# Q and K of a head pair in two row tiles from split operands, in a transformer block whose VectorE, ScalarE and TensorE orders are written by hand

## What is computed

```python
x = x + 0.5 * ffn(layernorm(x), w_gate, w_up, w_down)          # 128 -> 352 -> 128, silu(gate) * up
x = x + attn(layernorm(x), w_q, w_k, w_v, w_proj, b_proj, ln_gamma, ln_beta)
x = x + 0.5 * ffn(layernorm(x), w_gate, w_up, w_down)

# attn(x): 16 heads of 64
q, k, v = (split_heads(x @ w) for w in (w_q, w_k, w_v))
attn = softmax(einsum('bnqd,bnkd->bnqk', q, k) * 64 ** -0.5)
o = einsum('bnqk,bnkd->bnqd', attn, v)
y = o @ w_proj + b_proj + x;  y = layernorm(y, eps=1e-6) * ln_gamma + ln_beta
```

## Time and profile before

| | |
|---|---|
| Three runs | 2266.74, 2265.52, 2261.74 us, median 2265.52 |
| Profiled execution, its own time | 2263.16 us |
| Its span | 2261.4 us, 38387 instructions |
| TensorE matmul busy | 2142.7 us (95%) |
| VectorE, GpSimd, ScalarE busy | 1605.5, 1407.7, 1151.4 us (71%, 62%, 51%) |
| Mean granted TensorE clock | 0.978 |
| Costliest on TensorE | PV 552.3 us, Q and K 267.1 us, V 137.5 us, projection 126.7 us, row sums 68.2 us |

### The profile page before, as it was taken

The page is one execution under the profiler, slowest core; times in us unless marked ns, Lnnn a source line. Parts: engine busy times, 40 slices in busy tenths (PEclk is TensorE's granted clock), DMA queues, the critical chain, the costliest instruction groups (busy, mean ns, idle before and its releaser), DMA issues.

```text
span 2261.4 us, 38387 instructions
## 1 busy us (share of the span) xinstructions
PE 2142.7 (95%) x14537; PEld 1094.4 (48%) x14537; DVE 1605.5 (71%) x2609; ACT 1151.4 (51%) x1749; POOL 1407.7 (62%) x1289
## 2 busy tenths in 40 slices
PE   3899999999999999999999999999999999999974
PEld 2344444545445454545545454554544545454432
DVE  5565767767687786868777686877778687776634
ACT  2455554645555454555545455455555545454532
POOL 3365666757576675757756576675757667665642
PEclk8799999999999999999999999999999999999986
DMA  1000000000000000000000000000000000000000
GB/s 60 1 7 2 6 2 2 12 2 7 7 7 7 2 11 2 7 7 7 7 2 11 2 7 7 2 12 2 10 3 6 7 2 12 2 2 7 2 7 10
DMA packets 167493, 15.83 MB, mean 7 GB/s; under 512 B 148304, under 2 KB 166928, under 8 KB 167312
## 3 DMA queue, kind: packets, MB, share of 16 engines
q1 hardware_dynamic: 167312, 13.39, 5.1%
HBM read 7.03 MB, written 4.19 MB: 5 GB/s over the span
## 4 chain that ended last, share of the span: by engine, by line
PE 85%; DVE 6%; SPq 2%; issue 2%; POOL 2%; DMA 1%; ACT 1%; POOLq 0%; DVEq 0%
PE pS L934 23%; PE pO L961 20%; PE pM L918 9%; PE pX L946 5%; PE pM L1077 5%; PE pX L985 5%; PE pM L973 3%; PE LpF L333 2%; PE FpF L333 2%; SPq L568 2%; PE FpF L296 2%; PE LpF L296 2%; PE LpF L309 2%; PE FpF L309 2%; PE LpF L324 1%
## 5 line engine op out<-in xcount | busy, mean ns | idle before, releaser
L676 POOL TENSOR_TENSOR ES<-ES,E 128x512 f32<-128x512 f32 x512 | 654.9, 1300 | 217.1 <-ACT E L747 209.9
L747 ACT ACTIVATE E<-pS 128x1024 f32<-128x1024 f32 x512 | 523.2, 1022 | 459.9 <-PE pS L934 421.3
L799 DVE TENSOR_REDUCE nmax<-pX 128x2 fp32r<-128x1024 f32 x512 | 622.0, 1215 | 113.4 <-PE pX L946 98.4
L961 PE MATMUL pO<-E,VA 128*64 128x512 f32 x2048 | 552.3, 618 | 0.0
L670 POOL TENSOR_TENSOR ES<-E 128x512 f32<-128x512 f32 x256 | 321.9, 1279 | 247.5 <-ACT E L747 247.5
L918 PE MATMUL pM<-xf,w_raw 128*64 128x512 f32 x1024 | 267.1, 600 | 2.8 <-DVE QL L889 2.1
L934 PE MATMUL pS<-QH,KH 64*128 64x512 f32 x1024 | 255.9, 496 | 0.0
L946 PE MATMUL pX<-KH,QH 64*128 64x512 f32 x1024 | 241.0, 412 | 4.7 <-DVE nmax L799 3.3
L934 PEld LDWEIGHTS pS<-QH,KH 64*128 64x128 f32 x1024 | 95.5, 183 | 288.1 <-issue 269.3
L946 PEld LDWEIGHTS pX<-KH,QH 64*128 64x128 f32 x1024 | 186.3, 306 | 36.7 <-DVE nmax L799 8.0
L934 PE MATMUL pS<-SH,onesr 64*128 64x512 f32 x1024 | 203.6, 393 | 0.0
(11 more groups left out here) (178 smaller groups left out, 3000.0 us busy)
## 6 DMA issues: line engine op xcount, KB each, us to landing
RROW<-RC SPq DMA_DIRECT2D x512, 2.0 KB, 2.0
xin<-in_L_attn_x SPq DMA_DIRECT2D x16, 256.0 KB, 3.0
SH<-nmax SPq DMA_DIRECT2D x256, 2.0 KB, 2.0
LC<-LROW SPq DMA_DIRECT2D x256, 2.0 KB, 2.1
out<-X SPq DMA_DIRECT2D x16, 256.0 KB, 2.5
w_raw<-in_L_attn_w_q SPq DMA_DIRECT2D x1, 512.0 KB, 3.6
w_raw<-in_L_attn_w_k SPq DMA_DIRECT2D x1, 512.0 KB, 4.7
w_raw<-in_L_attn_w_v SPq DMA_DIRECT2D x1, 512.0 KB, 5.6
```

Source lines behind the costliest of these rows:

```text
L676: ins = g.tensor_tensor(ES[i % 3][:, hd, :], ES[i % 3][:, hd, :], E[s][:, hd, :], ALU.add)
L747: a.activation(E[s][:, :, :], pS[:, :, :], ACT.Exp).then_inc(s_exp, 1)
L799: v.tensor_reduce(nmax[px % 2][:, :, t:t + 1], pX[:, :, :], AX.X, ALU.max, negate=True).then_inc(s_max, 1)
L961: ins = pe_.matmul(pO[half(hd), :], VA[of][:, kt, j * 128 + 64 * hd:j * 128 + 64 * hd + 64], E[kt][:, hd, :], start=kt == 0, stop=kt == KT ...
```

## The change

Q and K are no longer formed one after the other from fp32 operands. The weights and the transposed input are split once into fp32r high and low parts (W and xs), and one function makes Q and K of a pair together: the product runs over 128 rows in two halves of 64, and while one half works for Q (into pM), the other works for K (into pO). Three products (high by high, high by low, low by high) make one turn of six matmuls; the second turn has the halves exchanged and waits for the end of the first. Both turns lie in s = 1, the first ahead of for_maxima, the second behind it. K now lies in pO until VectorE has read it, so PV(0) moves from s = 1 to s = 2, where two quarters stand behind each other. The V rounds move to s = 0 of seven pairs of a batch (and one to s = 3 of p = 0), straight behind PV; the projection and the row sums also come ahead of the layer pieces. QH, QL, KH, KL and OT are held three times in place of four, xf once, and the layers' tile xm becomes xn.

```diff
-        if s == 2:
-            return {-1: (0,), 0: (2,)}.get(i, ())
-        if s == 3:
-            return (1,) if i == -1 else (i + 3,) if 0 <= i < ROUNDS - 3 else ()
...
+    def v_place(r):
+        c, k = r // 8, r % 8
+        p, s = ((-2, 0), (-1, 0), (0, 0), (0, 3), (1, 0), (2, 0), (3, 0), (4, 0))[k]
+        return PAIRS * c + p, 3 if c == 0 and k < 2 else s
...
-        w_raw = m.sb("w_raw", [128, 3, NH * HD])
+        wv = m.sb("wv", [128, NH * HD])
+        W = [m.sb(f"W{k}", [128, 2, NH * HD], F32R) for k in ("hi", "lo")]
...
-        xf = [m.sb(f"xf{i}", [128, S]) for i in range(2)]
-        QH = [m.sb(f"QH{i}", [128, S], F32R) for i in range(4)]
+        xf = m.sb("xf", [128, S])
+        xs = [m.sb(f"xs{k}", [128, S], F32R) for k in ("hi", "lo")]
+        QH = [m.sb(f"QH{i}", [128, S], F32R) for i in range(3)]
...
```

On ScalarE and VectorE:

```diff
                     for c in batch_at(FirstLayer, FirstLayer.xf, b, t):
                         act.wait_ge(s_xmT_ps, c + 1)
-                        a.activation(xf[c % 2][:, :], F.pF[:, :], ACT.Copy).then_inc(s_xf, 1)
+                        a.activation(xs[0][:, :], F.pF[:, :], ACT.Copy)
+                        a.activation(xf[:, :], F.pF[:, :], ACT.Copy).then_inc(s_xf, 1)
...
+                    for c in batch_at(FirstLayer, FirstLayer.down, b, t):
+                        if c == 0:
+                            act.wait_ge(s_raw, 48)
+                            for k in range(2):
+                                a.activation(W[0][:, k, :], raw[k], ACT.Copy).then_inc(s_whi, 1)
...
-                        if s == 0 and there(i + 2, NP):
-                            act.wait_ge(s_q, i + 3)
-                            a.activation(QH[(p + 2) % 4][:, :], pM[:, :], ACT.Copy, scale=SCALE).then_inc(s_qhi, 1)
                         if s == 1 and there(i + 2, NP):
-                            act.wait_ge(s_k, i + 3)
-                            a.activation(KH[(p + 2) % 4][:, :], pM[:, :], ACT.Copy).then_inc(s_khi, 1)
+                            act.wait_ge(s_qk, i + 3)
+                            a.activation(QH[(i + 2) % 3][:, :], pM[:, :], ACT.Copy, scale=SCALE).then_inc(s_qhi, 1)
+                            a.activation(KH[(i + 2) % 3][:, :], pO[:, :], ACT.Copy).then_inc(s_khi, 1)
...
+                    for c in batch_at(FirstLayer, FirstLayer.xf, b, t):
+                        dve.wait_ge(s_xf, c + 1)
+                        v.tensor_tensor(xs[1][:, :], F.pF[:, :], xs[0][:, :].bitcast(F32), ALU.subtract).then_inc(s_xlo, 1)
+                    for c in batch_at(FirstLayer, FirstLayer.down, b, t):
+                        if c == 0:
+                            for k in range(2):
+                                dve.wait_ge(s_whi, k + 1)
+                                v.tensor_tensor(W[1][:, k, :], raw[k], W[0][:, k, :].bitcast(F32), ALU.subtract).then_inc(s_wlo, 1)
...
-                        if s == 0 and there(i + 2, NP):
+                        if s == 1 and there(i + 2, NP):
                             dve.wait_ge(s_qhi, i + 3)
...
-                        if s == 1 and there(i + 2, NP):
                             dve.wait_ge(s_khi, i + 3)
-                            v.scalar_tensor_tensor(KL[(p + 2) % 4][:, :], pM[:, :], 1.0, KH[(p + 2) % 4][:, :].bitcast(F32),
+                            v.scalar_tensor_tensor(KL[(i + 2) % 3][:, :], pO[:, :], 1.0, KH[(i + 2) % 3][:, :].bitcast(F32),
                                                    ALU.mult, ALU.subtract).then_inc(s_klo, 1)
```

On TensorE:

```diff
-                def per_head(k, p, x):
-
-                    for hd in range(2):
-                        ins = pe_.matmul(pM[half(hd), :], w_raw[:, k, p * 128 + 64 * hd:p * 128 + 64 * hd + 64], x,
-                                         start=True, stop=True)
-                    return ins
+                def query_key(i, p, turn):
+
+                    cols = slice(p * 128, p * 128 + 128)
+                    if turn == 1:
+                        pe.wait_ge(s_side, i + 1)
+                    for n, (w, x) in enumerate(((0, 0), (0, 1), (1, 0))):
+                        for side in range(2):
+                            k = (side + turn) % 2
+                            ins = pe_.matmul((pM, pO)[k][:, :], W[w][half(side), k, cols], xs[x][half(side), :],
+                                             start=turn == 0 and n == 0, stop=turn == 1 and n == 2)
+                    ins.then_inc(s_side if turn == 0 else s_qk, 1)
...
                         if kt == 0:
                             wait(pe, s_ot, i)
+                            pe.wait_ge(s_klo, min(i + 3, NP))
...
                     for s in range(KT):
                         if there(i, NP):
                             scores(i, p, s)
...
+                        if s == 1 and there(i + 2, NP):
...
+                            wait(pe, s_va, rounds_until(i, 0))
+                            wait(pe, s_ot, i)
+                            query_key(i + 2, (p + 2) % PAIRS, 0)
                         if s < 2:
                             for_maxima(i + 1, p + 1, s + 2)
                         else:
                             for_maxima(i + 2, p + 2, s - 2)
+                        if s == 1 and there(i + 2, NP):
+                            query_key(i + 2, (p + 2) % PAIRS, 1)
                         if s == 0:
                             times_v(i - 1, (p - 1) % PAIRS, KT - 1)
-                        else:
-                            times_v(i, p, s - 1)
+                        if s == 2:
+                            times_v(i, p, 0)
+                            times_v(i, p, 1)
+                        if s == 3:
+                            times_v(i, p, 2)
+                        for r in rounds_at(i, s):
+                            kt, of = r % 4, (r // 4) % 2
...
+                            ins.then_inc(s_v, 1)
                         if s == 1 and p % 2 == 1 and there(i - 4, NP):
                             project(i, p)
                         if s == 2 and p % 2 == 0 and there(i - 1, NP):
                             row_sums(i)
...
+                        first_ffn(b, 4 * p + s)
+                        last_ffn(b, 4 * p + s)
```

More of the change, by code:

```diff
@@ L470, in make_program @@
         ES = [m.sb(f"ES{i}", [128, 2, S]) for i in range(3)]
-        OT = [m.sb(f"OT{i}", [128, S]) for i in range(4)]
+        OT = [m.sb(f"OT{i}", [128, S]) for i in range(3)]
         ON = [m.sb(f"ON{i}", [128, S]) for i in range(2)]
@@ L496, in make_program @@
         s_pad = m.sem("s_pad")
+        s_whi = m.sem("s_whi")
+        s_wlo = m.sem("s_wlo")
         s_wT_ps = m.sem("s_wT_ps")
@@ L539, in make_program @@
         s_yacc = m.sem("s_yacc")
+        raw = [E[k][:, :, :].rearrange("p h n -> p (h n)") for k in range(2)]
         with nc.Block() as block:
@@ L730, in last_ffn @@
                     for c in batch_at(LastLayer, LastLayer.apply, b, t):
-                        norm_y.apply(nc, act, c, L.xm, Yacc[c % 2])
+                        norm_y.apply(nc, act, c, L.xn, Yacc[c % 2])
                     for c in batch_at(LastLayer, LastLayer.apply_x, b, t):
@@ L992, in first_ffn @@
                     for c in batch_at(FirstLayer, FirstLayer.turn_x, b, t):
-                        wait(pe, s_xf, c)
+                        wait(pe, s_xlo, c)
                         F.pe_x(pe, c)
@@ L1065, in body @@
                             row_sums(i)
-                        for r in rounds_at(i, s):
-                            kt, of, xb = round_place(i, p, bpar, r)
-                            pe.wait_ge(s_klo, min(i + 3, NP))
-                            wait(pe, s_va, r)
-                            if there(i - 3, NP):
-                                pe.wait_ge(s_norm, i - 2)
-                            elif i == 2:
-                                pe.wait_ge(s_lrow, 1)
-                            if p == 5:
-                                pe.wait_ge(s_xf, b + 2)
-                            for n in range(2):
-                                ins = pe_.matmul(pM[half(n), :], xf[xb][:, kt * 128 + 64 * n:kt * 128 + 64 * n + 64],
-                                                 w_raw[:, 2, of * S:of * S + S], start=True, stop=True)
-                            ins.then_inc(s_v, 1)
+                        first_ffn(b, 4 * p + s)
+                        last_ffn(b, 4 * p + s)
                 steps(pe, body)
```

85 lines of the change are left out of this document (42 added, 43 removed).

## The result

| | before | after |
|---|---|---|
| median, the two side by side | 2264.95 us (4 runs) | 2282.12 us (4 runs, 2280.07 to 2285.14) |
| profiled execution / span | 2263.16 / 2261.4 us | 2285.14 / 2283.4 us |
| TensorE busy | 2142.7 us, 14537 instructions | 2106.5 us, 15049 |

What follows compares the result with a forecast made beforehand. TensorE's program order was taken as the bound. Per batch -6.4 of gains and old waits and 8.4 of new waits, taken as 1.85 x 16 = +30: 2263.2 + 30 - 3 - 1 = 2289 us, range 2232 to 2318.

Steps and rivals of the forecast that it cites:

- QK pairs at 0.23: TensorE, s = 1: six matmul pairs at the scores' spacing, 1.40 us for 1.72; taken as -2.6 per batch.
- Rival C: TensorE's Q and K product: its weight loads lie bare, +146 us, 2435 us in all; chance 0.02.
- Projection behind the reduction: Odd p, s = 1: projection waits for the last reduction, 0.73 at t = 5 and 29, 1.6 at 13, 1.1 at 21.
- KH and KL, 2.4: Behind the second turn: pX waits for KH, PV(0) for KL; 1.05 each at t = 9, 25, 0.35 at 17.
- V moves from s = 3 ... to s = 0, a stage later, so this one goes: V rounds: moving them a stage later ends V's wait behind ON's broadcast, 12.7 us in the whole run before.
- Old waits, 3.0: TensorE, full batch of the kernel before: 132.87 against 129.9 counted out, so 3.0 are waits, uncertainty 0.5; all taken away.
- Prologue, -3: First Q to first scores: serial Q, QH, QL, K, KH becomes hi, lo, QK, QH, KH; -3 us, bounds -6 and +2.
- Tail, -1: End of the run: row sums come before a layer piece, -1 us.
- Rival A: Waits from a late queue (t = 8, 24, 27, parts at 13, 21; 3.1 per batch) vanish: faster, 2241 us; chance 0.22.
- Rival B: VectorE comes late in every s = 1, KL queued behind reduction and quantization: +51, 2340 us; chance 0.10.
- Rival D: Whole kernel: gain and waits cancel, 2259 to 2268 us; chance 0.06.
- Rival S: Set up for the experiments: waits are one slack of VectorE and ScalarE; one taken away comes back elsewhere; no chance given.

Runs made afterwards that it cites:

- Projection last: Changed kernel with the projection behind the layer pieces again in s = 1 of odd p: 2261.44 us, 0.9995 of the kernel before.
- K first: Changed kernel with KH made ahead of QH on ScalarE and KL ahead of QL on VectorE: 2271.31 us, 1.0038 of the kernel before.
- V in s = 3: Changed kernel with the V rounds back in s = 3 of each pair, straight behind PV: 2252.40 us, 0.9949 of the kernel before.
- pieces last: Kernel before with V, projection and row sums straight behind PV, Q and K, and the layer pieces behind them: 2259.18 us, ratio 0.9982.
- half reduction: Changed kernel with each reduction of pX taken over half of the keys: 2224.3 us, 0.9832 of the kernel before.
- order alone: Changed kernel with V rounds in s = 3, projection behind the layer pieces, KH and KL made first, no slot moved: 2226.32 us, ratio 0.9845.
- later rounding: Changed kernel with projection behind layer pieces, KH and KL first, moved slots, and the first layer's second rounding a stage later: 2214.27 us, ratio 0.9774.

## Why the prediction was right, and which steps were off

**The sign and the size** are right: +26 was forecast, +17.2 in the medians and +22.0 in the profiled executions were measured. The full batch was to be 134.7, and is 134.9.

**QK pairs at 0.23**: right for five of six. The first pair of the second turn takes 0.33, which adds 0.1 x 8 = 0.8 per batch: 1.9 gained, where the working took 2.6. The product is the term that was most mis-sized; the prediction's own sign of being wrong, pairs 0.3 apart, is met by this one pair in six. The row halves change places between the turns and pX lies between; which of the two costs the 0.1 was not tried. **The second turn's wait** on the first is free, as taken.

**Rival C**, bare loads, is out: at 0.19 a load, pairs could not follow each other at 0.23. The rule in the Trainium skill ("TensorE: Matmul & The Clock Gate", Part 3, "The mechanism") that a load overlaps only when its row group differs does not hold for these pairs, each of which reloads both halves (0.18 to 0.19 us a load in the changed kernel too); the opening of the same section, which lets a load into the background weight buffer go ahead as well, would allow them, and no run here shows which buffer they used.

**Projection behind the reduction, 4.2 per batch**: at t = 5 it starts at T+3.49 as worked out, and t = 29 takes the same 5.99. t = 13 waits 1.37 instead of 1.6: the reduction starts at T+2.81, not 3.0. The prediction's own terms, 2.61 + 0.86 - 0.69, give 2.78; the 3.0 was a slip in the sum. t = 21 waits 0.8 instead of 1.1. Sum 3.6. Projection last shows the cause by taking 1.7 of it away with no other change.

**KH and KL, 2.4**: t = 9 and 10 together take 8.37, with PV(0) 0.03 later than worked out; t = 25 and 26 take 7.89 (7.87 worked out), and PV(0) starts 0.33 late in t = 18 (0.35). Right; K first shows the part that is KL's.

**pX at t = 8 and 24, 1.0**: pX starts 0.57 and 0.31 late (0.7 and 0.3 taken), and each time 0.23 is added as its two matmuls start one after the other, which the working did not have. That makes 0.80 and 0.54, so 1.3. **The exp at t = 27, 0.8**: within 0.1 (0.72).

**The step that was wrong, though the total was right: "V moves from s = 3 ... to s = 0, a stage later, so this one goes".** The working let the move of V remove the wait behind ON. The move does remove it, but so do the other edits without it: with V in s = 3 the wait is 1.0 us in all. At t = 15, where six of the nine old waits lay, VectorE needs the same time from the reduction of t = 14 to ON; what grew is TensorE's stage t = 14, from 2.94 to 3.79, since PV(0) now stands in it. The kernel before, in a short batch, then the changed kernel with V in s = 3:

```profile
1055.61 1.23 DVE L799 TENSOR_REDUCE nmax<-pX 128x2 fp32r<-128x1024 f32 x1 [0.76 <-PE pX L946]
1056.98 0.50 PE L934 MATMUL pS<-QH,KH 64*128 64x512 f32 x2
...
1059.40 0.68 DVE L880 TENSOR_TENSOR ON<-OT,pM 128x512 f32<-128x512 f32 x1
```

```profile
1048.99 1.23 DVE L808 TENSOR_REDUCE nmax<-pX 128x2 fp32r<-128x1024 f32 x1 [0.76 <-PE pX L967]
1051.23 0.50 PE L955 MATMUL pS<-QH,KH 64*128 64x512 f32 x2
...
1052.80 0.68 DVE L897 TENSOR_TENSOR ON<-OT,pM 128x512 f32<-128x512 f32 x1
```

From reduction to ON it is 3.79 and 3.81; behind the scores ON starts at 2.42 and at 1.57. In both VectorE has stood idle for the projection just before, so QL's leaving s = 0 is not what made room. At t = 15 the credit belongs to the move of PV(0) into s = 2, and the move of V earned nothing. (That it is PV(0) is read from the timelines, no run moves it alone; that V's move was not needed is shown by V in s = 3.) V's move cost 2.1 per batch, 30 us in all and more than the whole slowdown. The waits that it opened (t = 8, 24, 28) were counted, one by one, but under other parts, and nowhere was the move itself added up. The total was right, because both halves were in it.

**Old waits, 3.0**: V behind ON was named among them, but in the batch that was counted V stands only 0.11 and 0.08 for it (t = 15 and 27), and TensorE's whole idle time there is 1.0, 0.63 of it the projection at t = 13. The rest of the 3.0 is small delays from start to start. What the sampled batch did not show is that some batches of before are 1.15 longer. Their stage t = 15, VectorE and TensorE (T is 922.98):

```profile
925.34 1.27 DVE L162 TENSOR_SCALAR ny_var<-ny_mv 128x4 f32<-128x4 f32 x1
...
926.53 0.67 DVE L880 TENSOR_TENSOR ON<-OT,pM 128x512 f32<-128x512 f32 x1
...
927.35 1.08 PE L1077 MATMUL pM<-w_raw,xf 128*64 128x512 f32 x4 [1.23 <-DVE ON L880]
```

An operation on 128x4 lasts 1.27 us where it mostly takes 0.17; ON comes late by that, and V waits 1.23. The stage takes 5.38, in the other batches 4.26. So the vanished wait was worth 0.4 per batch more (4 x 1.15 over twelve) than one batch showed, and that is why +1.64 came out and not +2.05. Added up, the new waits measure 3.6 + 2.6 + 1.3 + 0.7 = 8.2 (8.4 taken), so 6.6 went (6.4 taken) though the product gave 0.7 less than its term. 0.4 of what made up for it is these long batches; the rest, some 0.5, no reading here places. That two errors nearly cancel is luck in the size of the total, not in the path.

**Prologue, -3**: it was +0.3. From the down step (43.05 in the earlier trace rows, 45.22 now) to the first scores it is 34.85 us, before 36.74: -1.9 (33.2 in projection last and 35.0 in K first, so it has some 2 us of play). The 2.2 ahead of that step, where nothing was changed, are gate products that follow each other at 1.18, before at 0.59; the granted clock is 1.00 over them in both traces, so the rows don't say why. It is a matter of the execution and not of the kernel: projection last, with the changed prologue, has its down step at 42.93, and the kernel before with its pieces last has 45.29. Short of -3 it fell because QK0 waits for the low part of x, 1.90 us of idle time, as transposes, xs high, xf and xs low follow one another (columns as in the earlier trace rows):

```profile
59.09 0.79 PE L941 MATMUL pM<-xshi,Whi 64*128 64x512 f32 x1 [1.90 <-DVE xslo L837]
...
76.37 0.82 PE L969 MATMUL pX<-KH,QH 64*128 64x512 f32 x2 [2.67 <-DVE nmax L810]
```

and because pX at 76.37 waits 2.67 for a reduction behind VectorE's other work. **Tail, -1**: up to the last down step but one it is -0.9, as worked out; from there it is +2.4, at a lower granted clock: that step lasted 5.39 us at a clock of 0.50, the 1.2 GHz level (2235 to 2245 us), before 4.03 at 0.62 (2215 to 2225). Executions differ by as much: from the first scores of the last batch to the end it is 202.6 in the changed kernel and 200.7 before, but 200.0 in K first and 202.1 in the kernel before with its pieces last. The medians differ by 17.2 and the profiled executions by 22.0.

**Rival A** (waits from a late queue vanish, 2241) had 0.22: they did not vanish, as the waits at t = 8, 13 and 27 show. **Rival B** (VectorE late in every s = 1, 2340) is out: at t = 5 and 9 VectorE stands idle 1.3 and 1.2 before the reduction. **Rival D** (gain and waits cancel) is out by 14 us. **Rival S** falls by the half reduction, which lowers the time by 58 us and leaves KH's and KL's waits at the same 11.0 and 14.5, and by order alone: V 2.1 and the two others 1.8 per batch add to the 3.9 that the three give together. Only with later rounding did its number come true.

## What to carry to other kernels

When a product is made shorter on the engine that sets the pace, the work that it hid comes bare: list for each wait what stood between producer and consumer, and put something that waits for nothing back there. Here that was an order of issue inside the stage (layer pieces ahead of the projection, the split that is wanted first made first, V ahead of the scores whose maxima are late), and it turned +0.8% into -1.5% without moving a layer piece to another stage. If a move is credited with the end of a wait, ask whether the wait would end without it.

## What the runs showed that I had not expected

Small VectorE operations can last as long as a GpSimd instruction beside them. In the trace of the kernel before, 102 of the 320 TENSOR_SCALAR operations on 128x4, 128x32 or 128x44 last longer than 0.3 us, up to 1.7, and the others 0.16 to 0.20. Each of the 102 ends 0.03 to 0.05 us behind the end of a GpSimd instruction, nearly always an addition of the row sums (1.27 us); in the changed kernel that is so for all 88 long ones. The short ones begin with none of these additions running, no more than 17 ns behind the start of one, or so near its end that they outlast it anyway. So such an operation that begins while the addition runs goes on until that ends. These two traces show no exception for the additions; no run takes them away. It does not hold for every GpSimd instruction: in the trace of half the reduction 26 short ones lie whole within one that forms nx_rstd (L168).

Between the long and the short batches of before, some 10 ns decide. Taken to the ns, ny_var starts 2 to 17 ns behind the start of an addition in nine batches and takes 0.16 to 0.17; it starts 23 or 24 ns behind it in five and takes 1.27. Four of these five are the four full batches of 134.0 us (the fifth is the last but one). The long one above, at 925.34, and the short one of the earlier trace rows:

```profile
925.32 2.49 POOL L676 TENSOR_TENSOR ES<-ES,E 128x512 f32<-128x512 f32 x2 [0.40 <-ACT E L747]
...
1059.33 2.53 POOL L676 TENSOR_TENSOR ES<-ES,E 128x512 f32<-128x512 f32 x2 [0.42 <-ACT E L747]
1059.33 0.17 DVE L162 TENSOR_SCALAR ny_var<-ny_mv 128x4 f32<-128x4 f32 x1
```

ScalarE's KH started 0.50 us after QH (1045.86 and 1046.36 above), though QH is shown as 0.60 long: the two step by 0.1 less than the first lasts. The working added the full 0.60, and met KH's end only because QH began 0.1 later than worked out.
